# Sorting 103125 edge rows in a fused GNN kernel: 63 of 188 clearing transfers kept, the padding rows written by 57 indexed transfers inside the scatter

## The reference, cut to what matters

```python
msg_input = jnp.concatenate([node_feats[dst], edge_feats], axis=1)
h = leaky_relu(msg_input @ msg_w1 + msg_b1)
messages = h @ msg_w2 + msg_b2
aggregated = jax.ops.segment_sum(messages, src, num_segments=node_feats.shape[0])
```

## Time and profile before

| | us |
|---|---|
| median of 3 runs | 3380.08 (3377.29 to 3383.94) |
| the profiled execution | 3380.8 |
| its span, first to last instruction | 3379.1 |
| prologue, to the first instruction of block 2 | 181.0 |
| wait of POOL for the clears, ending at | 280.2 |
| last row transfer issued at | 1309.5 |
| first instruction of the edge stage | 1318.8 |

### The profile page before, as it was taken

One profiled execution on the slowest core, in us unless ns is written; L12 is line 12 of the kernel. 1 busy time (PEld: TensorE's weight loads), 2 busy tenths in 40 slices (PEclk: granted clock), 3 DMA queues, 4 the chain that ended last, 5 costly groups with the idle time before them and its releaser, 6 DMA issues. The chain is left out here.

```text
span 3379.1 us, 87741 instructions
## 1 busy us (share of the span) xinstructions
PE 2511.1 (74%) x20390; PEld 1974.6 (58%) x20391; DVE 2597.0 (77%) x8325; ACT 1489.4 (44%) x3942; POOL 1952.3 (58%) x2344
## 2 busy tenths in 40 slices
PE   1433555555555554999999999999999239989899
PEld 1322334333334343999999999999997214445455
DVE  7863777777777773999999999999997779983501
ACT  2011222222222222677777777777775655452200
POOL 1005777777777777899999999999996000000000
PEclk9975677677777776999999999999999559999999
DMA  9993222222222223888888888888886669869766
GB/s 381 414 414 129 78 78 83 78 78 78 77 79 78 78 68 104 236 240 234 242 239 235 240 239 234 242 238 236 241 239 226 255 282 343 301 219 315 249 220 208
DMA packets 738172, 696.84 MB, mean 206 GB/s; under 512 B 48524, under 2 KB 637275, under 8 KB 734779
## 3 DMA queue, kind: packets, MB, share of 16 engines
q1 hardware_dynamic: 516770, 536.77, 47.6%
q10 hardware_dynamic: 195544, 104.71, 12.7%
q0 software_dynamic: 25792, 54.52, 4.9%
HBM read 340.91 MB, written 354.90 MB: 206 GB/s over the span
## 5 line engine op out<-in xcount | busy, mean ns | idle before, releaser
L855 POOL DMA_INDIRECT sorted_rows<-rows,posi x806 | 785.1, 974 | 338.7 <-issue 221.4
L1147 DVE SCALAR_TENSOR_TENSOR acc<-acc,keep,pm 128x256 f32<-128x256 f32 x1504 | 715.7, 476 | 70.9 <-issue 23.9
L965 POOL TENSOR_SCALAR ohs_e<-iota,rt 128x128 f32<-128x128 f32 x1128 | 666.2, 607 | 12.4 <-DMA rt<-sorted_rows 12.4
L803 PE MATMUL s_peq<-sb_w1bb,eT 128*128 128x256 f32 x806 | 352.5, 531 | 398.9 <-ACT eT L658 379.9
L1074 PE MATMUL pm<-ohw_e,ohs_e 128*128 128x128 f32 x3008 | 609.1, 283 | 0.0
L974 POOL TENSOR_TENSOR hid<-pre_e,excess 128x512 f32<-128x512 f32 x376 | 482.8, 1284 | 117.2 <-ACT excess L1001 117.2
L1080 PE MATMUL px<-PN,dT 128*128 x4512 | 498.1, 219 | 0.4 <-ACT dT L1014 0.4
L1020 ACT ACTIVATE ohw_e<-ohd_e,rt 128x128 f32<-128x128 bf16 x1504 | 490.5, 397 | 0.0
L1074 PEld LDWEIGHTS pm<-ohw_e,ohs_e 128*128 128x128 f32 x3008 | 461.8, 194 | 0.0
L803 PEld LDWEIGHTS s_peq<-sb_w1bb,eT 128*128 128x128 f32 x806 | 172.8, 265 | 441.1 <-ACT eT L658 432.7
L1091 PE MATMUL ps<-hid,ohs_e 128*128 128x129 f32 x3008 | 424.3, 283 | 0.5 <-POOL hid L974 0.5
(11 more groups left out here) (317 smaller groups left out, 4206.3 us busy)
## 6 DMA issues: line engine op xcount, KB each, us to landing
count_matrices<-acc SPq DMA_DIRECT2D x1504, 128.0 KB, 2.6
sorted_rows<-zrow SPq DMA_DIRECT2D x188, 528.0 KB, 10.5
rt<-sorted_rows ACTq DMA_DIRECT2D x184, 528.0 KB, 4.6
gab<-count_matrices SPq DMA_DIRECT2D x60, 1280.0 KB, 6.0
arb<-count_matrices SPq DMA_DIRECT2D x25, 1664.0 KB, 8.8
ab<-count_matrices SPq DMA_DIRECT2D x25, 1600.0 KB, 9.3
arb<-count_matrices SPq DMA_DIRECT2D x25, 1536.0 KB, 8.5
ef<-in_edge_attr_dram SPq DMA_DIRECT2D x58, 364.0 KB
```

The source lines that it names most:

```text
L803: nc.tensor.matmul(pe_q[:, q % 2, 0:2 * D], eT[:, q % 2, :], w1bb[:], start=True, stop=True).then_inc(s_q, 1)
L855: pool.indirect_dma_start(sortd, bass.IndirectOffsetOnAxis(ap=posi[:, h, c:c + 1], axis=0), rows[:, h, c, :], None).then_inc(s_sc[h], 16)
L965: last = nc.gpsimd.tensor_scalar(ohs[:, k % BUFS, j, :], iota128[:], rt[:, k, j, D + 1:D + 2], None, ALU.is_equal)
L1147: nc.vector.scalar_tensor_tensor(acc[:, k % SUMS, j, :], before, keep[:, at:at + 1] if isinstance(at, int) else keep[:, ds(at, 1)], pm[:, ...
```

## The change

- The array `sorted_rows` is divided at tile 1000 (`EDGE`). Only the 504 tiles from there on are cleared as before: 63 transfers, 46 in block 1 and 17 in block 2. They start after the index arrays and the node features have landed. POOL waits for these 63.
- Below tile 1000 only the padding rows are written: the end of each bin's last tile, cut into blocks of 32 rows (up to four) and one block each of 16, 8, 4, 2 and 1. DVE works out the indices at the end of the prologue; a block that a bin does not have, or that lies beyond tile 1000, gets an index out of bounds, which the transfer skips. There are 45 such transfers (9 sizes by 5 groups of 125 bins), 4 for the tiles that fill a source tile's run up to a multiple of four (75 blocks each) and 8 for tiles that no bin uses (100 blocks each), 57 in all. POOL issues one ahead of the 13 row transfers of a half, from the fifth half on. `zrow` grows from 8 to 32 rows a partition. POOL's loop over bodies is written out.
- The tables (L427 to L453 before) move from the prologue into seven bodies of the scatter on DVE, in pieces of six instructions; the copy to DRAM goes with them, and the loads of the tables to the last body.
- The node projections and their split into three parts move from the prologue to the end of block 2, behind the last edge features; ACT takes two of the four steps, and the bias is one matrix product per four tiles.
- The prologue's one-hots are all 16-bit, with the column as the innermost index, 52 columns at a time; weights are loaded by SP; ACT does copies that DVE did.
- The first edge features are loaded by SP, and POOL no longer clears `ef` and all of `rows`.

The core of the diff:

```diff
+BLK = 32
+PARTS2 = (16, 8, 4, 2, 1)
+EDGE = 1000
+FREE = 100
+PADP = 125
...
+            BLIND = EDGE // ZR
+            CLEARED = 46
...
-                    with sp.Fori(0, CLEARED) as n:
+                    sp.wait_ge(s_xl, 32)
+                    sp.wait_ge(s_ix, 16 * 9)
+                    with sp.Fori(BLIND, BLIND + CLEARED) as n:
...
-                        nc.vector.tensor_tensor(ohs[:, n % 2, 0:w, :], iota32[:].unsqueeze(1).to_broadcast([P, w, QP]),
-                                                tile[:, 1, c].unsqueeze(2).to_broadcast([P, w, QP]), ALU.is_equal)
+                        nc.vector.tensor_tensor(ohs[:, n % 2, :, 0:w], rep32[:, :, 0:w],
+                                                tile[:, 1, c].unsqueeze(1).to_broadcast([P, QP, w]), ALU.is_equal)
...
+                    for i in range(2, 2 + PIECES):
+                        begin(i, 0, False)
+                        positions(i - 1, 1, False)
+                        places(i, 0)
+                        tables(i - 2)
...
+                    pe.wait_ge(s_cq, BODIES * PAIRS)
+                    for g in range(NQ):
...
-                    pool.wait_ge(s_zd, 16 * (TT // ZR))
+                    pool.wait_ge(s_zd, 16 * (TT // ZR - BLIND))
+                    def clear(index, parts, size):
+                        spots = sortd.rearrange("(n s) w -> n (s w)", s=size)
+                        pool.indirect_dma_start(
+                            spots, bass.IndirectOffsetOnAxis(ap=index, axis=0),
+                            zrow[0:parts, 0:size, :].rearrange("p k w -> p (k w)"), None,
+                            bounds_check=EDGE * P // size - 1, oob_is_err=False).then_inc(s_cl, 16)
+                    def padding(n):
+                        if n < NPAD * COLS:
+                            k, c = n // COLS, n % COLS
+                            clear(padi[:, k, c:c + 1], PADP, BLK if k < WHOLE else PARTS2[k - WHOLE])
+                        elif n < NPAD * COLS + WHOLE:
+                            c = n - NPAD * COLS
+                            clear(fulli[:, c:c + 1], 3 * NT, BLK)
+                        else:
+                            c = n - NPAD * COLS - WHOLE
+                            clear(freei[:, c:c + 1], FREE, BLK)
...
                             if c == 0:
+                                n = i * 2 + h - AFTER
...
+                                if 0 <= n < PIECES_OF_PADDING:
+                                    padding(n)
```

More of the change, by code:

```diff
@@ new lines, in _ @@
+                @block.scalar
+                def _(act):
+                    act.wait_ge(s_pd, 1)
+                    act.dma_start(X[:, 0:NT - 1, :], x[0:(NT - 1) * P, :].rearrange("(t p) d -> p t d", p=P)).then_inc(s_xl, 16)
+                    act.dma_start(X[0:NR, NT - 1, :], x[(NT - 1) * P:N, :]).then_inc(s_xl, 16)
+                    act.wait_ge(s_z, 2)
+                    for k in range(1, BLK // ZR):
+                        nc.scalar.activation(zrow[:, k * ZR:(k + 1) * ZR, :], zrow[:, 0:ZR, :], ACT.Copy)
@@ new lines, in _ @@
+                    for n in range(NS):
+                        counts(n)
+                        if n == 1:
+                            act.wait_ge(s_ln["stats"], 2)
+                        for t in range(max(2 * n - 2, 0), min(2 * n, NT)):
+                            nc.scalar.activation(H[:, t, :], X[:, t, :], ACT.Relu, bias=nbias[:, t:t + 1],
+                                                 scale=rstd[:, t:t + 1]).then_inc(s_ln["h"], 1)
+                    for g in range(NQ):
+                        turned(g)
@@ L505, in _ @@
                     nc.tensor.matmul(wt[:, 3, 0:NT], same[0:NT, :], cnt[:, 4, :], start=False, stop=True).then_inc(s_tp, 1)
-                    for g in range(2, NQ):
-                        project(g)
-                    pe.wait_ge(s_dv, 4)
-                    for k, row in enumerate((0, 1, 3, 2)):
-                        last = nc.tensor.transpose(tt[:, k, :], table[:, row, :], ident[:])
-                    last.then_inc(s_tp, 1)
             with ExitStack() as ctx:
@@ L749, in _ @@
                     places(1, 1)
-                    with dve.Fori(2, BODIES) as i:
+                    for i in range(2, 2 + PIECES):
[3 more added lines that the diff above has]
+                        tables(i - 2)
+                        begin(i, 1, False)
+                        positions(i, 0, False)
+                        places(i, 1)
+                    with dve.Fori(2 + PIECES, BODIES) as i:
                         begin(i, 0, False)
@@ L857, in step @@
                                 rows[:, h, c, :], None).then_inc(s_sc[h], 16)
-                    step(0)
-                    with pool.Fori(1, BODIES) as i:
+                    for i in range(BODIES):
                         step(i)
+                    pool.wait_ge(s_cl, 16 * PIECES_OF_PADDING)
                     for h in range(2):
```

496 lines of the change are left out of this document (299 added, 197 removed).

## The result

The changed kernel takes 3305.1 us, the median of four runs (3301.4 to 3311.3), beside 3379.5 for the kernel before on the same chip: a ratio of 0.978, with a 95% interval of 0.976 to 0.980. The forecast was 3284, its range 3255 to 3335. The profiled execution, the longest of the four, took 3311.3 us with a span of 3309.5; 27.5 us of the gain that the sum promised are not there (21.3 by the median). In the profile, line 1014 is the row transfer (855 before), line 978 the block transfer, lines 279 and 627 the blind clears of the two blocks.

A forecast was written before the change was run, and what follows sets the result against it. Clears set POOL's start, then POOL's transfers set the pace, with the edge stage unchanged: 3380.8 - 172 (earlier start) + 73 (block transfers) + 2 (end) = 3283.8 us. Range 3255 to 3335; the forecast's own, 3255 to 3307.

The forecast's parts named there:

- What bounds the kernel: Up to the edge stage: start of the scatter plus number of POOL's transfers times the step, 1.279 us.
- rival A: Prologue's one-hots stay at one element a cycle, block 1 ends 23.6 us later, time 3307; chance 8%.
- Start of the scatter: POOL waits for 63 clears instead of 188 and starts at 108 instead of 280.2 us, a gain of 172.
- I take 12: Block 1: inputs landed at 12 us, between about 10 by bytes and the 14.5 seen before.
- 26.3 + 2: Block 2: 10.9 MB of edge features and clears take 26.3 us at 415 GB/s, some 2 to land.
- POOL's extra transfers: Scatter: 57 block transfers on POOL, each priced like a row transfer at 1.279 us, add 73 us.
- The lower bound, by valid indices: Block transfers: only the 40% valid indices cost POOL, 0.68 us each, 39 us in all.
- rival C: POOL's time goes by packet-sized pieces: block transfers cost 307 us instead of 73, time 3518; chance 7%.
- Hidden work: Scatter: DVE's table pieces fit its step, and ACT's 9.4 us wait covers the largest block transfer's data; no loss.
- rival D: Block data goes over few of 16 engines: no loss at five engines, 75 us at half that rate, 3359; chance 5%.
- End: End of the scatter: node projections finishing around POOL's end cost +2 us, between 0 and +5.
- rival B: Bounds check or longer pieces double POOL's work per block transfer: 127 us instead of 73, time 3338; chance 14%.

The follow-up runs named there:

- experiment 6: Two kernels against experiment 2: blind clearing from tile 1056 instead of 1000 alone, 3285.1 us; the same with 64-row blocks, 3270.1 us.
- experiment 1: The changed kernel without the 13 block transfers that carry no valid index, the other 44 kept: 3281.6 us.
- experiment 2: The changed kernel with 128 instead of 125 indices in the 45 block transfers by bins: 3291.8 us.
- experiment 5: Blocks of 64 rows instead of 32 on top of experiment 2, 46 block transfers instead of 57: 3278.4 us.
- Experiment 4: The changed kernel's first block, but all 188 blind clears and no block transfers: 3385.0 us, 1.0021 against the kernel before.
- experiment 7: The changed kernel with tile numbers in 32 instead of 16 bits, so one-hots compare a 32-bit operand: 3325.4 us.
- experiment 8: 64-row blocks, 128 indices, edge at tile 1056, and the node-feature addition moved from after the first to after the last projection: 3265.5 us.

## Why the prediction was right, and by what it was short

- **What bounds the kernel: right.** The last clear sets POOL's start (experiment 6, and the 1.0 us in every trace), POOL's transfers the stretch behind it (experiments 1, 2, 5), and the edge stage is unchanged to 0.5 us. Experiment 4 gives the scatter without blocks at 1031.4 and so confirms 1.28 a step.
- **The number: inside its range, with parts at the edge of theirs.** The 3305.1 lies inside the forecast's own range, 3255 to 3307, but POOL's start at 116.05 lies outside its 103 to 115 and the block transfers' 83.6 at the end of their 55 to 85; both miss the same way. The time is also that of rival A, 3307. Only the one-hots' rows and experiment 7 tell the two apart.
- **Start of the scatter: right order, 8.0 short.** "I take 12" for the inputs failed: they landed at 16.95, 5 later, although no clears ran beside them. The step behind it, bytes at the clears' 415 GB/s, failed: the DMA engines were busy all the time and moved less, and the weights that SP now loads there were not among the 2.8 MB.

```profile
9.00:13.00 4.00, 0.00 (x0) 0.00 (x0) 0.00 (x0) 3.47 (x4) 3.92 (x22) 1.00 1.04 261
```

  The compares' price was right, 1.02 and 0.83 us, though with DVE's waits for PE a round took 1.99 instead of 1.86. The block's start came at 82.8 instead of 79.5, since counts and index arithmetic took 7.2 instead of 9.6 and made up for part. From there the sum by bytes, 26.3 + 2, took 33.3: SP needed from 82.8 to 89.4 to issue the features, with the DMA engines at 152 GB/s from 80 to 90, and the last clear landed 6.7 us after its issue. The 172 were 164.1.
- **The rows: right.** The places at 97.8 and the second pair of columns copied by 103.1 (102.5 was forecast); the clears decide, by 13 us instead of 5.
- **POOL's extra transfers: the mechanism right, the size 10.6 short.** The failed step is "125 indices are about as many as 128". The price is not one of indices: 125 cost 1.205 us, 128 of the same blocks 0.996 (experiment 2). At 128 the 57 would have been 74.3, the forecast's 73. The lower bound, by valid indices, is refuted by experiment 1, and rival C, by packets, by blocks of 32 rows and of one row at the same price.
- **Hidden work: right but for two things.** The landing of the large blocks took 20.8 us, above the half's 17.9, and the packets ran on few engines, so rival D's first half happened. The cover held: the landings stay at 19.6 to 21.8 over nine such transfers, ACT's mean wait at 524.8 / 59 = 8.9, and the rival's "no loss" came out right, but for the 6.64 of the one wait that not every execution has. With experiment 2's quick landing the row steps take 1033.5 instead of 1041.2, of which 6.3 are that wait. The other thing was in no sum: the addition to the node features, 3.48 us on DVE, had moved into the scatter, and held one of POOL's transfers.
- **End: 0 instead of +2.** The projections end before POOL does; the bound "once for four tiles" was the right one.
- **Rival A** was worth 20.3, not 23.6, mainly since the 16-bit rounds ran at 1.99 us and not 1.86; **rival B**'s 127 is too high by 43.4.

## What to carry to other kernels

Where an engine's queue sets the pace, price what is added to it by the instruction and not by its bytes, and choose the shape of an indirect transfer as carefully as its count: 125 indices cost 0.2 us more than 128, and the large blocks took nearly three times as long to land. A start that waits for "the last of many transfers" is set by landing and not by issue; a burst's last landing must be read from the trace. When work moves into a stretch that one engine bounds, list every instruction that comes along, also those on other engines.

## Hardware that the runs showed and I had not expected

- Void indices are not free: a transfer with none of its 125 or 100 indices in bounds takes POOL 1.205 or 1.005 us, like one with 97 valid.
- The last of a burst of equal clears lands 6.6 to 16.5 us after its issue, in the long bursts several us later than those before it (15.1 after 10.7, 16.5 after 6.1).
- An indirect transfer of 125 indices had at most 5 of its large packets running at a time, one of 128 up to 18.
- An instruction of DVE can hold up POOL's issue of a transfer: beside the addition of 3200 elements from two operands in SBUF (1217.73 to 1221.21) one row transfer took 3.43 us instead of 0.96; without it (experiment 8) none above 1.40. The Trainium skill, page "SBUF — State Buffer", section "Terms", says that the two share a pair of ports that one holds for a whole instruction. The trace agrees for this instruction: the transfer ended 0.8 us after the addition, whose own 3.48 us are the same in experiment 8. On a smaller scale, four transfers issued well within additions of line 867 (0.68 us each, both operands in SBUF) took 1.12 to 1.18 us.
